# Building P on GpSimd, V's sines in PSUM, and a second keep-warm of TensorE in a vision-tower kernel

## What is computed

```python
# token mixing: a diagonal state-space kernel of length 512
dt = jnp.exp(log_dt)
Cc = C[..., 0] + 1j * C[..., 1]
w = -jnp.exp(log_w_real) + 1j * w_imag
dtA = w * dt[:, None]
K = dtA[:, :, None] * jnp.arange(L)
Cm = Cc * (jnp.exp(dtA) - 1.0) / w
h = 2 * jnp.einsum('chn,hnl->chl', Cm, jnp.exp(K)).real
# then, on h:
h = h + attention(layernorm(h), w_q, w_k, w_v, w_o)   # 16 heads, 4 key heads, rotary, causal
h = h + ffn(layernorm(h), ...)                        # 8 experts chosen by a gate of low rank
```

## Time and profile before

| | us |
|---|---|
| median of 3 runs | 841.18 (841.08 to 843.98) |
| the profiled execution's own time | 840.35 |
| its span (first to last instruction) | 838.6 |
| PE busy | 746.5 (89%) |
| DVE busy | 587.1 (70%) |
| ACT busy | 453.9 (54%) |
| POOL busy | 436.3 (52%) |
| first matmul of the mixing starts | 46.65 |
| last matmuls of the mixing end | 105.28 |
| first projection of the attention starts | 120.67 |

### The profile page before, as it was taken

One profiled execution on the slowest core, in us unless ns is written; L12 is line 12 of the kernel. 1 busy time (PEld: TensorE's weight loads), 2 busy tenths in 40 slices (PEclk: granted clock), 3 DMA queues, 4 the chain that ended last, 5 costly groups with the idle time before them and its releaser, 6 DMA issues.

```text
span 838.6 us, 19677 instructions
## 1 busy us (share of the span) xinstructions
PE 746.5 (89%) x6944; PEld 682.8 (81%) x6944; DVE 587.1 (70%) x1631; ACT 453.9 (54%) x1246; POOL 436.3 (52%) x657
## 2 busy tenths in 40 slices
PE   0066778899999999999999999999999999999985
PEld 0055757799999999999999999999999998899762
DVE  7979957777775665666666656666655777777877
ACT  6633316555555656555565565555756644554420
POOL 0076934555554746444447464444747566556522
PEclk9998988899999999999999999999999999999996
DMA  9013460100010102000001020000100000000002
GB/s 207 0 41 63 84 242 25 39 2 0 0 33 6 51 2 76 0 0 0 0 1 51 1 77 0 0 0 0 37 16 2 1 2 26 25 25 25 1 25 75
DMA packets 30533, 26.46 MB, mean 32 GB/s; under 512 B 22476, under 2 KB 22860, under 8 KB 30228
## 3 DMA queue, kind: packets, MB, share of 16 engines
q1 hardware_dynamic: 30196, 25.71, 10.7%
q10 hardware_dynamic: 288, 0.13, 0.1%
HBM read 17.44 MB, written 8.39 MB: 31 GB/s over the span
## 4 chain that ended last, share of the span: by engine, by line
PE 78%; DVE 13%; issue 3%; POOL 3%; ACT 2%; DVEq 0%; DMA 0%; SPq 0%; ACTq 0%
PE bank L1199 17%; PE bank L1201 17%; PE bank L1200 17%; PE bank_pair L1201 4%; PE bank_pair L1199 4%; PE bank_pair L1200 4%; POOL w_lo L421 2%; DVE bank_pair L887 2%; PE bank L1339 2%; PE bank_pair L1339 2%; PE bank_pair L1349 1%; PE bank L1353 1%; PE bank L1349 1%; PE bank L1292 1%; PE bank L1211 1%
## 5 line engine op out<-in xcount | busy, mean ns | idle before, releaser
L1199 PE MATMUL bank<-xt_hi,w_hi 128*128 (+1 forms) x768 | 216.6, 282 | 1.6 <-POOL w_lo L421 0.8
L1201 PE MATMUL bank<-xt_lo,w_hi 128*128 (+1 forms) x768 | 214.4, 279 | 0.0
L1200 PE MATMUL bank<-xt_hi,w_lo 128*128 (+1 forms) x768 | 214.3, 279 | 0.0
L968 DVE TENSOR_TENSOR kq<-bank,cst 128x512 f32<-128x512 f32 (+1 forms) x96 | 57.9, 603 | 140.2 <-ACT swap L655 106.6
L466 POOL TENSOR_TENSOR swap<-swap,cst 128x512 f32<-128x512 f32 (+1 forms) x96 | 105.7, 1103 | 81.5 <-ACT swap L655 80.0
L1199 PEld LDWEIGHTS bank<-xt_hi,w_hi 128*128 128x128 f32 x768 | 144.3, 188 | 3.0 <-issue 1.6
L1201 PEld LDWEIGHTS bank<-xt_lo,w_hi 128*128 128x128 f32 x768 | 144.2, 188 | 0.0
L1200 PEld LDWEIGHTS bank<-xt_hi,w_lo 128*128 128x128 f32 x768 | 144.1, 188 | 0.0
L349 POOL TENSOR_TENSOR spare<-cst 1x1 f32<-1x1 f32 x87 | 16.6, 191 | 226.4 <-DVE rinv L1102 141.2
L695 ACT ACTIVATE sm<-sm,mx 128x128 f32<-128x128 f32 (+1 forms) x256 | 113.6, 445 | 21.7 <-DVE mx L1092 21.6
L654 ACT ACTIVATE swap<-bank 64x512 f32<-64x512 f32 (+1 forms) x96 | 50.3, 523 | 124.9 <-PE bank L1201 122.1
(11 more groups left out here) (251 smaller groups left out, 1922.7 us busy)
## 6 DMA issues: line engine op xcount, KB each, us to landing
mixed<-st SPq DMA_DIRECT2D x32, 128.0 KB, 2.0
out<-x SPq DMA_DIRECT2D x16, 256.0 KB, 2.1
raw<-in_w_qkv SPq DMA_DIRECT2D x8, 384.0 KB, 3.5
raw<-in_w_o SPq DMA_DIRECT2D x10, 256.0 KB, 2.5
x<-mixed SPq DMA_DIRECT2D x2, 1280.0 KB, 10.2
norm_mem<-in_w_qkv SPq DMA_DIRECT2D x6, 384.0 KB, 3.7
x<-mixed SPq DMA_DIRECT2D x3, 512.0 KB, 4.7
norm_mem<-in_w_o SPq DMA_DIRECT2D x6, 256.0 KB, 2.9
```

Source lines behind the costliest of these rows:

```text
L968: v.tensor_tensor(view(kq), src, table(cosT), ALU.mult).then_inc(kq_cos, 1)
L1199: mmul(dst, lh, rh, start=start and k == 0, stop=False, skip_group_check=True)
L1200: mmul(dst, ll, rh, start=False, stop=False, skip_group_check=True)
L1201: last = mmul(dst, lh, rl, start=False, stop=stop and k == n - 1, skip_group_check=True)
```

## The change

It has six parts.

1. **Loads.** The two loads of `log_dt` become one, the load of `w_im` moves from ScalarE's queue to SyncE's and gets a semaphore of its own (`wim_in`), for which VectorE waits only at `turn`.
2. **V in PSUM.** ScalarE writes V's sines into PSUM banks 0 to 3 (`v_trig`), and VectorE multiplies from there. The order on VectorE becomes U, the D chain, V.
3. **P on GpSimd.** GpSimd multiplies P by its magnitudes, in two halves, and makes a quarter of P times D: the real part of the second half of the poles. VectorE makes the other three quarters: both parts of the first half before step 0, the imaginary part of the second half before step 6. The D factors that VectorE reads there lie in PSUM (`d_first`, `d_rest`).
4. **G behind each B.** In steps 0 and 1 VectorE makes B then G for step 0, then B and G for step 1.
5. **Warm-up.** TensorE runs `keep_warm(5)` as soon as V is done, before step 0, and `keep_warm(7)` in place of `keep_warm(5)` at the join.
6. **Gate constants first.** GpSimd waits for the twelve gate constants (`pw_done`) before the first `split_lo`.

```diff
-        banks = [top.enter_context(nc.psum_tensor(f"bank{k}", [P, 512], F32)) for k in range(4)]
+        quad = top.enter_context(nc.psum_tensor("bank_quad", [P, 4, 512], F32))
+        banks = [quad[:, k, :] for k in range(4)]
...
-        d_rest = [tmp[:, 1024 - (k + 1) * 64:1024 - k * 64] for k in range(3)]
+        d_first = tmp[:, 512:512 + 192].rearrange("p (k e) -> p k e", k=3)
+        d_rest = tmp[:, 896:1024].rearrange("p (k e) -> p k e", k=2)
+        v_trig = quad[:].rearrange("p k e -> p (k e)").rearrange("p (q r e) -> p q r e", q=NQ, r=2)
...
-            for hh in range(2):
-                sp.dma_start(lg[hh * NS:(hh + 1) * NS, 0, :],
-                             log_dt[hh * P:(hh + 1) * P].unsqueeze(0).to_broadcast([NS, P])).then_inc(par_in, 16)
+            sp.dma_start(lg[:, 0, :], log_dt.rearrange("(hh h) -> hh h", hh=2).unsqueeze(1).to_broadcast(
+                [2, NS, P])).then_inc(par_in, 16)
+            sp.dma_start(wim[:], w_im).then_inc(wim_in, 16)
...
+            pool.wait_ge(d_poles, 1)
+            pool.wait_ge(trig_ready, 4)
+            for k in range(2):
+                qs = slice(k * HALF_Q, (k + 1) * HALF_Q)
+                m = mag[:, 2].rearrange("p (q h) e -> p q (h e)", q=NQ)[:, qs].unsqueeze(2).to_broadcast(
+                    [P, HALF_Q, 2, 64])
+                nc.gpsimd.tensor_tensor(ptab[:, qs], ptab[:, qs], m, ALU.mult).then_inc(p_mag, 1)
+
+            def per_pole(t):
+                return t[:, HALF_Q * QH8:].rearrange("p (q h) -> p q h", q=HALF_Q).unsqueeze(3).to_broadcast(
+                    [P, HALF_Q, QH8, LE])
+
+            second = slice(HALF_Q, NQ)
+            grid = lambda t: t.rearrange("p q (h e) -> p q h e", h=QH8)
+            pool.wait_ge(p_mag, 2)
+            nc.gpsimd.tensor_tensor(grid(pq[2][:]), grid(ptab[:, second, 0, :]), per_pole(dr), ALU.mult)
+            nc.gpsimd.tensor_tensor(grid(pq[3][:]), grid(ptab[:, second, 1, :]), per_pole(ndi), ALU.mult).then_inc(pool_prod, 1)
+            pool.wait_ge(pool_prod, 1)
+            nc.gpsimd.tensor_tensor(pa[:, second, 0, :], pq[2][:], pq[3][:], ALU.add).then_inc(pa_pool, 1)
+
...
+            pool.wait_ge(pw_done, KC)
...
-            trig(0, vtab)
+            trig(0, v_trig)
...
-                act.wait_ge(pa_done, 2 * k + 2)
+                act.wait_ge(pa_done, k + 2)
+                if k:
+                    act.wait_ge(pa_pool, 1)
...
-            dve.wait_ge(par_in, 64)
+            dve.wait_ge(par_in, 32)
...
+            dve.wait_ge(wim_in, 16)
...
-            dve.wait_ge(trig_ready, 1)
-            times_mag(vtab, 0).then_inc(v_done, 1)
-            dve.wait_ge(trig_ready, 2)
+            dve.wait_ge(trig_ready, 3)
+            times_mag(utab, 1).then_inc(u_done, 1)
...
-            rest = slice(HALF_Q * QH8, P)
-            for k, d in enumerate((dr, ndi, ndr)):
-                last = v.tensor_copy(d_rest[k], d[:, rest])
-            link(last)
-            dve.wait_ge(trig_ready, 3)
-            times_mag(utab, 1).then_inc(u_done, 1)
-            dve.wait_ge(trig_ready, 4)
-            times_mag(ptab, 2).then_inc(p_mag, 1)
-
-            def p_times_d(k):
...
+            v.tensor_copy(d_first, dd[:, :, 0:HALF_Q * QH8]).then_inc(d_poles, 1)
+            link(v.tensor_copy(d_rest, dd[:, 0:2, HALF_Q * QH8:]))
+            m = mag[:, 0].rearrange("p (q h) e -> p q (h e)", q=NQ).unsqueeze(2).to_broadcast([P, NQ, 2, 64])
+            v.tensor_tensor(vtab[:], v_trig, m, ALU.mult).then_inc(v_done, 1)
+
+            other = banks[4].rearrange("p (q e) -> p q e", q=HALF_Q)
+
+            def p_times_d(k, r, a, b):
...
-                re, im = grid(ptab[:, qs, 0, :]), grid(ptab[:, qs, 1, :])
-                d_re, nd_im, nd_re = d_rest if k else [d[:, 0:HALF_Q * QH8] for d in (dr, ndi, ndr)]
-                other = banks[4].rearrange("p (q e) -> p q e", q=HALF_Q)
-                for r, (a, b) in enumerate(((d_re, nd_im), (nd_im, nd_re))):
-                    v.tensor_tensor(grid(pq[r][:]), re, spread(a), ALU.mult)
-                    v.tensor_tensor(grid(other), im, spread(b), ALU.mult).then_inc(p_prod, 1)
-                    dve.wait_ge(p_prod, 2 * k + r + 1)
-                    v.tensor_tensor(pa[:, qs, r, :], other, pq[r][:], ALU.add).then_inc(pa_done, 1)
-                    if r == 0:
-                        dve.wait_ge(pa_done, 2 * k + 1)
+                v.tensor_tensor(grid(pq[r][:]), grid(ptab[:, qs, 0, :]), spread(a), ALU.mult)
+                v.tensor_tensor(grid(other), grid(ptab[:, qs, 1, :]), spread(b), ALU.mult).then_inc(p_prod, 1)
+                dve.wait_ge(p_prod, 2 * k + r + 1 - (1 if k else 0))
+                v.tensor_tensor(pa[:, qs, r, :], other, pq[r][:], ALU.add).then_inc(pa_done, 1)
 
             dve.wait_ge(p_mag, 1)
-            p_times_d(0)
+            p_times_d(0, 0, d_first[:, 2], d_first[:, 0])
+            dve.wait_ge(pa_done, 1)
+            p_times_d(0, 1, d_first[:, 0], d_first[:, 1])
...
             for s in range(2):
                 grid_b(s, s, s)
                 sum_b(s, s)
-            for s in range(2):
                 grid_g(s, s)
             for lo, hi in ((1, TURN_AT), (TURN_AT, NQ // 2)):
                 if lo == TURN_AT:
                     dve.wait_ge(b_ready, 2 * TURN_AT)
-                    p_times_d(1)
-                    dve.wait_ge(pa_done, 4)
+                    dve.wait_ge(p_mag, 2)
+                    p_times_d(1, 1, d_rest[:, 0], d_rest[:, 1])
+                    dve.wait_ge(pa_done, 3)
+                    dve.wait_ge(pa_pool, 1)
...
+            pe.wait_ge(cst_in, 16)
+            pe.wait_ge(v_done, 1)
+            keep_warm(5)
...
             pe.wait_ge(evac, NQ)
-            keep_warm(5)
+            keep_warm(7)
```

More of the change, by code:

```diff
@@ L197, in tower @@
         prods = ExitStack()
-        pq = [sb(f"pq{k}", [P, HALF_Q, 64], F32, prods) for k in range(2)]
+        pq = [sb(f"pq{k}", [P, HALF_Q, 64], F32, prods) for k in range(4)]
         prods.close()
@@ L1220, in lead, with keep_warm @@
                 mmul(banks[2 * s][:, 4 * P - 2:4 * P], pair(g1), pair(bt)[:, 0:2], start=True, stop=True, skip_group_check=True)
+            def keep_warm(count):
+                for _ in range(count):
+                    mmul(banks[0][:], ident, cst[:, 0:512], start=True, stop=True)
+            pe.wait_ge(cst_in, 16)
+            pe.wait_ge(v_done, 1)
+            keep_warm(5)
             for s in range(2):
@@ L1241, in _ @@
             last.then_inc(cw_mm, 1)
-            def keep_warm(count):
-                for _ in range(count):
-                    mmul(banks[0][:], ident, cst[:, 0:512], start=True, stop=True)
             pe.wait_ge(evac, NQ)
-            keep_warm(5)
+            keep_warm(7)
             def transpose_tokens(m, first_bank=5):
```

24 lines of the change are left out of this document (11 added, 13 removed).

## The result

The changed kernel takes **833.48 us** (median, 832.69 to 834.84) against 841.29 (841.08 to 843.98) before, a ratio of 0.9914, interval [0.9885, 0.9944]. The forecast was 830.8 with a range of 828 to 836. The profiled execution took 833.84 with a span of 832.0, so on the scale on which the sum was made 6.5 us came of the 10.4 expected.

A forecast was written before the change was run, and what follows sets the result against it. It took the start of TensorE's attention as decisive, set by VectorE until 46.65. Gains 0.6 + 5.3 + 3.4 + 1.1 = 10.4 us took 840.35 to 829.95; the median's 0.83 made 830.8, range 828 to 836.

The forecast's parts named there:

- Loads: At the start: with one `log_dt` load VectorE begins up to 1.0 us sooner, taken as 0.6.
- no wait for `p_times_mag`: In front, VectorE: a sign of being right was that `p_times_mag` is not waited for by more than 0.2 us.
- three products at the turn: Before step 6: three instructions of 0.69 us leave VectorE's queue, so three remain between steps 5 and 6.
- gate constants at 0.24: At the join: VectorE's gate constants no longer collide with GpSimd and take 0.2 us each.
- Step 0: In front: TensorE starts at 43.1 instead of 46.65 and VectorE starts step 2 5.3 us earlier.
- steps 2 to 5: Mixing loop after the front: expected unchanged, 13.7 us as before.
- rival A: Clock stays low or falls in new pauses: 1.6 us at step 0, 1.4 at step 6, 1.7 at join; 835.5; chance 0.20.
- Turn: Before step 6: pause shrinks to 3.5 us, clock stays up, wait before step 8 goes; 3.4 us, or 2.05 if it falls.
- Join: Before the first projection: transposes start at 116.85 instead of 118.0, 1.1 us gained, or 0.6 lost if the clock falls.
- B: In front: GpSimd and VectorE block each other, step 0's G up to 6.4 us later, gain 4.0, 837.2; chance 0.09.
- C: Attention: TensorE enters at the low clock and stays there, adding about 17 us, 848, slower than before; chance 0.03.
- D: Token load or first attention steps: the front's gain is lost again, no change, 841; chance 0.04.

The follow-up runs named there:

- h1_old_loads: The changed kernel with the two `log_dt` loads on SyncE and `w_im` on ScalarE's queue again: 833.68 us, ratio 0.9902.
- e1_front8: The changed kernel with keep_warm(8) in place of keep_warm(5) before step 0: 835.29 us, ratio 0.9931.
- e2_turn3: The changed kernel with TensorE's matmul loop split before step 6 and keep_warm(3) put there: 833.83 us, ratio 0.9909.
- e3_join11: The changed kernel with keep_warm(11) in place of keep_warm(7) at the join: 833.41 us, ratio 0.9909.
- g1_v_sbuf: The changed kernel with V's sines in SBUF again instead of PSUM, and the loads of the kernel before: 835.54 us, ratio 0.9928.

## Why the prediction was right, and by how much it was off

**Direction and place were right.** The moves in the order did what was predicted: V 2.29 beside GpSimd 2.33 (2.4 forecast), no wait for `p_times_mag`, first G at 39.82 (39.4), TensorE at 42.94 (43.1 on the old scale, 42.5 with the loads' 0.6), three products at the turn, gate constants at 0.24, transposes released by the tokens. Of the parts that were tried alone only the loads were a loss.

**Four terms were too large**, 4.2 in all up to the first copy of a projection, which came 6.2 earlier (117.50 against 123.67) where 10.4 were forecast:

- *Loads*, 0.6 forecast and -0.3 measured, so 0.9 short. The sum counted only the issues of `log_dt`; the load that VectorE then waits for is the one on ScalarE's queue. h1_old_loads puts the old start back.
- *Step 0*, 5.3 forecast and 4.8 measured from VectorE's start, so 0.5 short, of which 0.3 came back in steps 2 to 5 (13.42 instead of 13.71). The pause lay inside the forecast 2 to 3 us, and the clock fell 1 us behind it. That was bad luck of this execution: in seven others with the same front it held. Nor is its price the 1.6 of rival A. It is 0.8 at step 2 (41.68 against 40.86), and nothing at step 6, since with the clock held steps 1 to 3 run into the pauses at their fixed places in the code (57.88 in e1_front8, 57.82 in h1_old_loads, against 57.54). The prediction had no term for these pauses, though the trace of before shows one, of 0.75 in step 3.
- *Turn*, 3.4 forecast and 2.05 measured, so 1.4 short. The failed step is "I expect the clock to stay up, since it was still full after 4.0 us without a matmul". The row was of one pause; that the clock was full at 4.0 in one execution did not say that it would be in another. In this trace it fell some 2.4 us after the last matmul of step 5, and it fell before or in step 6 in every profile that leaves the pause. e2_turn3 gives the 1.45 locally.
- *Join*, 1.1 forecast and -0.7 measured (from 6.84 gained at step 8 to 6.17 at the first copy), so 1.8 short, against the 1.7 that rival A names. e3_join11 shows 1.7 there; beside the shortest joins of the same code it would be 0.7. In that execution 1.1 was lost again in the first attention step.

So rival A, held at 0.20, was what happened: regularly at the turn and at the join, and at step 0 in this execution. Its price was right at the turn, right but at the upper end at the join, and twice too high at step 0. That the forecast came out inside its range is due to a range that reached over A, and to two smaller strokes of luck. Step 0 cost less than A said, and the median lies 0.4 below the profiled execution, where for before it lay 0.8 above. That swing of 1.2 brought the result nearer to 830.8 than the mechanism earned.

The rule of the Trainium skill that the prediction cites ("TensorE: Matmul & The Clock Gate", "What's actually happening": the window runs freely, tied to no matmul) agrees with these runs: pauses of 2.76 and 1.93 in front lost the clock, pauses of 2.50 (g1_v_sbuf) and 2.29 (h1_old_loads) kept it. What was wrong was the weight: where a rule says that a pause can fall either way, three pauses at 0.20 together are too cheap.

**B** was refuted for this kernel and shown for its neighbour (g1_v_sbuf: 2.0 us). **C** did not come: the clock was back before 116, after less than 6 us of matmuls, and a second low stretch in the first attention step was shorter than before (3.4 us against 6.8). **D** did not either: 6.2 of the gain went through the join and 6.6 were there at the end.

**Still open**: what TensorE waits for at the fixed places in its code, why those of the second loop cost nothing, and why the clock falls in one pause and not in a longer one. The profile gives the events but not their cause.

## What to carry to other kernels

Price every pause of some us that a change leaves on TensorE at the low clock unless work fills it. Then ask what holds the next stretch: the full clock at step 0 gained 0.8 at step 2 and nothing at step 6. Before you explain a difference of one or two us, look at the same stretch in several executions of the same code: here the join varied by 1.0 and what follows it by 3.0. On the first pass through long unrolled code TensorE may stop in mid-stretch, always behind the same record. If work waits there, fold the first steps into the loop that repeats them, and see that the warm-up run in front does not end late. When a product moves to GpSimd, keep one operand of VectorE's simultaneous product in PSUM: the same pair cost 2.0 us more without it.
